# Loading a turn's tile numbers into registers in two halves, in front of their first use

## The chip, the cores and the metric

The kernel runs on one core of a Trainium2 chip. The metric is the device time of the whole program in microseconds (us). Times are medians over runs; a profile is one execution recorded by the hardware profiler. Engines are written as in the profile: PE is TensorE (PEld its weight loads), DVE is VectorE, ACT is ScalarE, POOL is GpSimd, SP is SyncE. A q behind an engine (PEq, PEldq, DVEq, SPq) marks what its sequencer does itself: register work, branches, waits, DMA issues.

## The reference

A graph network of two layers over 6250 nodes with 128 features and 206250 edges. The first layer is a graph attention layer. The second, which the change is about, is this:

```python
msg = jnp.concatenate([x[row], x[col], edge_attr], axis=-1)
h = jax.nn.relu(msg @ W1 + b1)
msg_out = h @ W2 + b2
out = jax.ops.segment_sum(msg_out, row, num_segments=x.shape[0])
```

Here `row` is the source and `col` the target of an edge, and the result is added to x. The kernel splits `msg @ W1` into three parts (source row, target row, edge attributes), and sums the rows after the relu by source node before it multiplies them by W2.

## The kernel before

The program runs in stages. A node stage and an attention stage fill the first 2.2 milliseconds. A target stage then walks the edges in the order of their targets, computes the target and attribute part of each edge's row, and scatters the rows into a table `xr` in DRAM, grouped by the tile of 128 nodes to which the edge's source belongs. Each group is rounded up to 256 rows, so that every block of 256 rows (a pair of 128-row blocks, PR = 2) has sources in a single tile.

The source stage, which the change touches, reads `xr` back in order. There are NPAIR = 856 pairs, eight to a turn (SB = 8), and NTURN = 107 turns. All engines run the same loop over turns, each with its own part, and are tied together by semaphores:

- SP loads two pairs at a time (516 KB) into one of four slots of the buffer `XR` (L423, `load_xr`). The load for a slot waits until ACT has done the relu of the pairs that held it.
- DVE builds the one-hot matrices of a pair (`hotp`, L1342; for the first pair of a slot it also makes the gather's indices, L1333), adds the source part out of PSUM to the pair's rows in XR (`add_r`, L1350), and adds the pair's sums to the running sum of its node tile, `accB[reg]` (`add_up`, L1356).
- PE turns the one-hot matrices (`turnp`, L1679), multiplies them by the node tile's rows `Pt[reg]`, kept as three bf16 parts (`source_rows`, L1688: three matmuls for the second pair of a slot, six for the first), and multiplies the relu's rows by the one-hot matrix to sum them by node (`segment`, L1698: two f32 matmuls, each of which the profile shows as two).
- ACT copies the turned one-hots out of PSUM (L764), widens the other one-hots to f32 (L771) and computes the relu (`relu`, L780).
- POOL adds, for the second block of each second pair, the source part by an indirect DMA from `p_tab` (`source_add`, L556).

PE's loop is staggered: in step m of a turn it runs `turnp(m)`, `source_rows(m-1)`, `segment(m-3)`. DVE's runs `hotp(m+1)`, `add_r(m-2)`, `add_up(m-4)`. ACT's runs the copies of pair m and `relu(m-2)`.

Which node tile a pair belongs to is known only at run time. The numbers stand in one row of on-chip memory, `pbrow`, with four words of zeros ahead of them, so that word p + 4 belongs to pair p. PE and DVE need the number in a register to address `Pt[reg]` and `accB[reg]`. `pair_bins` (its load is L252 in the profile, an instruction TENSOR_LOAD) reads SB + 4 = 12 words at the head of each turn on both engines, the four numbers before the turn and the turn's own eight. PE uses 8 of the 12 (`regs[m + 3]`), DVE the first 8 (`regs[m]`). The loop's own branch and counter are L1712 on PE and L1372 on DVE. A helper of the same kind, `bins` (L246), reads 26 words a batch in the attention stage on PE and DVE; SP reads 7 words at a time at L318.

Of the kernel before, what the change touches and what calls it, by code (L numbers as in the profile page):

```python
# [10 lines left out]
ENG = mybir.EngineType  # L11
# [9 lines left out]
NT = -(-N // P)  # L21
# [23 lines left out]
SB = CP * NS  # L45
NPAIR = -(-((E + NT * (GR - 1)) // GR) // SB) * SB
NTURN = NPAIR // SB
# [18 lines left out]
def gnn(nc, x, src, dst, ea, W, asrc, adst, bias, W1, b1, W2, b2, out):  # L66
# [12 lines left out]
    with ctx:  # L79
# [4 lines left out]
        def sem(name):  # L84
            if name not in sems:
                sems[name] = ctx.enter_context(nc.semaphore(name))
            return sems[name]
# [126 lines left out]
        pbrow = Region(PB0, E1)([NPAIR + 16], I32, 1)  # L214
# [14 lines left out]
        def flat(v):  # L229
            d = dims(len(v.shape) - 1)  # L230
            return v.rearrange(f"p {d} -> p ({d})") if len(v.shape) > 2 else v
# [12 lines left out]
        def bins(engine, b, count):  # L244

            return nc.values_load_multi_w_load_instructions(  # L246
                bin_row[0:1, bass.ds(b * RB, count)], engines=[engine], min_val=0, max_val=NT - 1,
                skip_runtime_bounds_check_because="a node's tile, clamped at 0")[1]

        def pair_bins(engine, i):  # L250

            return nc.values_load_multi_w_load_instructions(  # L252
                pbrow[0:1, bass.ds(i * SB, SB + 4)], engines=[engine], min_val=0, max_val=NT - 1,
                skip_runtime_bounds_check_because="counted over the bins, held under their number")[1]


# [544 lines left out]
        def _(dve):  # L801
# [236 lines left out]
            def add_up(b, t, regs):  # L1038
                dve.wait_ge(sem("agg_ready"), b * BT + t + 1)
                dve.wait_ge(sem("acc_done"), b * (BT + 1) + 2 + t)  # L1040
                a = flat(acc[:, bass.ds(regs[t], 2), :])
                V.tensor_tensor(a, a, PSB[3 + t % 2][:, 0:2 * H * MW], ALU.add).then_inc(sem("acc_done"), 1)  # L1042
# [285 lines left out]
            def hotp(i, m, first):  # L1328
                s, k, g = m // CP, m % CP, SB * i + m
                if k == 0:  # L1330
                    dve.wait_ge(sem(f"xr_in{s}"), 16 * (i + 1))
                    n = len(NADD[s])
                    V.tensor_scalar(sidx[:, s, CP - n:], XR[:, s, CP - n:, RW + HID + 1], 0.0, None, ALU.max).then_inc(sem("idx_ready"), 1)  # L1333
                if not (first and m < 4):
                    dve.wait_ge(sem("pT_ps"), g - 3)
                    dve.wait_ge(sem("ohp_ready"), g - 3)
                if not first:
                    dve.wait_ge(sem("seg_ps"), g - SB + 1)
                for j in range(PR):
                    c, direct = j * RW + HID, j and added(s, k)  # L1340
                    o = OHp[:, m, j, :] if direct else OHq[:, m % 4, j, :]
                    last = V.tensor_scalar(o, iota[:, 0:P] if direct else iotab[:, 0:P], XR[:, s, k, c:c + 1], None, ALU.is_equal)  # L1342
                last.then_inc(sem("ohq_ready"), 1)

            def add_r(g, m, first):
                s, k = m // CP, m % CP
                dve.wait_ge(sem("pp_ps"), g + 1)
                n = PR - added(s, k)
                v = XR[:, s, k, :].rearrange("p (j w) -> p j w", j=PR)[:, 0:n, 0:HID]
                V.tensor_tensor(v, v, PSB[2 + m % 2][:].rearrange("p (j h) -> p j h", j=PR)[:, 0:n, :], ALU.add).then_inc(sem("hp_ready"), 1)  # L1350
# [5 lines left out]
                V.tensor_tensor(a, a, PSB[4 + m % 2][:, 0:XW], ALU.add).then_inc(sem("accB_done"), 1)  # L1356

            def sources(i, first=False, last=False):
                regs = pair_bins(ENG.DVE, i)
                for m in range(SB):  # L1360
                    if m < SB - 1:
                        hotp(i, m + 1, first)
                    else:
                        if not last:
                            hotp(i + 1, 0, False)
                    if not (first and m < 2):
                        add_r(SB * i + m - 2, (m - 2) % SB, first)
                    if not (first and m < 4):
                        add_up(SB * i + m - 4, (m - 4) % SB, regs[m])
            hotp(0, 0, True)  # L1370
            sources(0, True)
            with dve.Fori(1, NTURN - 1) as i:  # L1372
                sources(i)
            sources(NTURN - 1, last=True)
            regs = pair_bins(ENG.DVE, NTURN)
            for m in range(SB - 4, SB):
                if m < SB - 2:
                    add_r(NPAIR - SB + m + 2, m + 2, False)
# [21 lines left out]
        def _(pe):  # L1400
# [92 lines left out]
            regs = bins(ENG.PE, 0, BT)  # L1493
# [10 lines left out]
            regs = bins(ENG.PE, 1, BT)  # L1504
# [171 lines left out]
            def turnp(g, m):  # L1676
                pe.wait_ge(sem("ohq_ready"), g + 1)
                for j in range(PR - added(m // CP, m % CP)):
                    last = pe.transpose(PSB[m % 2][:].bitcast(BF16)[:, j * P:(j + 1) * P], OHq[:, m % 4, j, :], identb)  # L1679
                last.then_inc(sem("pT_ps"), 1)  # L1680

            def source_rows(g, m, reg, first):
                pe.wait_ge(sem("pT_ready"), g + 1)
                if not (first and m < 2):
                    pe.wait_ge(sem("hp_ready"), g - 1)
                for j in range(PR - added(m // CP, m % CP)):
                    for part in range(3):
                        last = pe.matmul(PSB[2 + m % 2][:, j * HID:(j + 1) * HID], ohTp[:, m % 2, j, :],  # L1688
                                         flat(Pt[:, bass.ds(reg, 1), part, :]), start=(part == 0), stop=(part == 2))
                last.then_inc(sem("pp_ps"), 1)  # L1690

            def segment(g, m, first):
                pe.wait_ge(sem("ohp_ready"), g + 1)
                pe.wait_ge(sem("hid_ready"), g + 1)
                if not (first and m < 2):
                    pe.wait_ge(sem("accB_done"), g)
                for j in range(PR):
                    last = pe.matmul(PSB[4 + m % 2][:, 0:XW], OHp[:, m, j, :], hid[:, m % 2, j, :], start=(j == 0), stop=(j == PR - 1))  # L1698
                last.then_inc(sem("seg_ps"), 1)

            def sources(i, first=False):
                regs = pair_bins(ENG.PE, i)
                for m in range(SB):
                    turnp(SB * i + m, m)
                    if not (first and m < 1):
                        source_rows(SB * i + m - 1, (m - 1) % SB, regs[m + 3], first)
                    if not (first and m < 3):
                        segment(SB * i + m - 3, (m - 3) % SB, first)
            pe.wait_ge(sem("pb_in"), 16)
            pe.wait_ge(sem("lo_ready"), NT)  # L1710
            sources(0, True)
            with pe.Fori(1, NTURN) as i:  # L1712
                sources(i)
            regs = pair_bins(ENG.PE, NTURN)
            source_rows(NPAIR - 1, SB - 1, regs[3], False)
            for m in range(SB - 3, SB):
                segment(NPAIR - SB + m, m, False)
            pe.wait_ge(sem("accB_done"), NPAIR + 1)
# [44 lines left out]
```

## Time and profile before

| | |
|---|---|
| median of 3 runs | 5817.26 us (5815.58 to 5819.93) |
| span of the profiled execution, first to last instruction | 5814.8 us |
| source stage, from the first to the last loop branch of PE | 4472.5 to 5770.8 us, 105 turns |
| busy in the span | PE 89%, PEld 70%, DVE 69%, ACT 50%, POOL 68% |
| TensorE's granted clock in the source stage | 1.00 |

The profiler gives no other time for the profiled execution than its span. The span lies inside the runs' times, about 2.5 us under their median. Register, branch, semaphore and DMA-issuing instructions are not counted as busy, so what a sequencer does shows only where a line or an idle gap is looked up.

### The profile page before, as it was taken

To read this page: it belongs to the slowest core of one execution; us is meant where nothing else is said; L and a number is where in the kernel's file an instruction comes from. 1 tells how busy PE (TensorE), PEld (TensorE's weight loads), DVE (VectorE), ACT (ScalarE), POOL (GpSimd) and SP (SyncE) were. 2 spreads that over 40 slices of the span, in tenths; PEclk is the share of its full clock that TensorE was granted. 3 is DMA by queue.
4 is the path that set the end of the run, shared out by engine and by line. 5 is a ranking of instruction groups with operands and counts; after the bars stand their busy time and mean duration, and the time that the engine had idled before them with its cause. 6 is when DMAs were issued, how large, how long until landed. Compare 5 with 4: busy or idle time off the path is not lost.

```text
span 5814.8 us, 160505 instructions
## 1 busy us (share of the span) xinstructions
PE 5152.1 (89%) x34498; PEld 4062.4 (70%) x34499; DVE 3991.1 (69%) x14406; ACT 2887.5 (50%) x8241; POOL 3967.9 (68%) x3713
## 2 busy tenths in 40 slices
PE   4888888888888886999999999999997999999999
PEld 3777777777777764776666666666665777777777
DVE  6788788778778777554455455544545888888887
ACT  3555555555555553333333333332224777777776
POOL 4777777777777774777777777777776555555543
PEclk6888898888888887999999999999998999999999
DMA  4422222222222244998888898888886998999997
GB/s 109 160 53 52 53 52 52 53 52 53 52 53 52 53 118 135 278 264 255 251 253 252 253 256 253 253 259 251 256 252 183 214 213 212 213 214 216 214 210 190
DMA packets 859988, 990.83 MB, mean 170 GB/s; under 512 B 307992, under 2 KB 663224, under 8 KB 859774
## 3 DMA queue, kind: packets, MB, share of 16 engines
q1 hardware_dynamic: 662494, 608.23, 39.9%
q0 software_dynamic: 190592, 378.22, 23.8%
q10 hardware_dynamic: 6816, 3.38, 0.2%
q8 instruction: 37, 0.61, 0.0%
q14 instruction: 49, 0.40, 0.0%
HBM read 726.65 MB, written 262.76 MB: 170 GB/s over the span
## 4 chain that ended last, share of the span: by engine, by line
PE 59%; POOL 11%; issue 11%; DMA 10%; DVE 5%; ACT 2%; DVEq 1%; POOLq 0%; ACTq 0%; SPq 0%
PE bank L1698 13%; PE bank L1530 12%; PE bank L1621 8%; PE bank L1623 7%; PE bank L1688 7%; DMA xr<-arena 7%; POOL arena L494 6%; POOL xr L542 5%; PE bank L1456 2%; DMA arena<-h_tab,arena 2%; PE bank L1679 1%; PE bank L1611 1%; PE bank L1592 1%; PE bank L1466 1%; DVE arena L935 1%
## 5 line engine op out<-in xcount | busy, mean ns | idle before, releaser
L542 POOL DMA_INDIRECT xr<-arena x1612 | 1623.5, 1007 | 511.9 <-issue 383.3
L494 POOL DMA_INDIRECT arena<-h_tab,arena x1612 | 1601.5, 994 | 543.8 <-issue 406.3
L1530 PE MATMUL bank<-arena 128*128 128x136 f32 x6448 | 1321.1, 334 | 76.4 <-DVE arena L1042 9.0
L703 ACT ACTIVATE arena<-bank 128x256 f32<-128x256 f32 x1612 | 594.5, 385 | 1443.1 <-PE bank L1623 986.2
L1621 PE MATMUL bank<-arena 128*128 128x256 f32 x3224 | 1040.1, 405 | 109.8 <-DVE arena L1236 62.0
L556 POOL DMA_INDIRECT arena<-p_tab,arena x428 | 667.8, 1560 | 660.2 <-DMA arena<-p_tab,arena 427.5
L1530 PEld LDWEIGHTS bank<-arena 128*128 128x128 f32 x6448 | 989.2, 216 | 160.5 <-issue 62.1
L621 ACT ACTIVATE arena<-bank 128x256 bf16<-128x256 bf16 x1612 | 618.4, 384 | 922.4 <-PE bank L1456 848.8
L1623 PE MATMUL bank<-arena 128*128 128x256 f32 x3224 | 986.1, 388 | 0.0
L1698 PE MATMUL bank<-arena 128*128 128x257 f32 x3424 | 898.2, 384 | 3.9 <-ACT arena L780 2.7
L1042 DVE TENSOR_TENSOR arena<-arena,bank 128x272 f32 x1612 | 690.7, 428 | 169.5 <-PE bank L1530 156.5
L1236 DVE TENSOR_SCALAR arena<-arena 128x128 f32<-128x128 bf16 x1612 | 464.6, 304 | 448.9 <-PE bank L1623 432.5
L1621 PEld LDWEIGHTS bank<-arena 128*128 128x128 f32 x3224 | 550.4, 203 | 214.5 <-issue 85.9
L1623 PEld LDWEIGHTS bank<-arena 128*128 128x128 f32 x3224 | 631.2, 196 | 91.8
L628 ACT ACTIVATE arena<-arena 128x256 f32<-128x256 bf16 x1612 | 644.9, 408 | 24.9 <-PE bank L1530 21.8
L1698 PEld LDWEIGHTS bank<-arena 128*128 128x128 f32 x3424 | 585.5, 191 | 75.5 <-issue 5.9
L780 ACT ACTIVATE arena<-arena 128x512 f32<-128x512 f32 x856 | 535.5, 626 | 97.1 <-DVE arena L1350 75.0
L1688 PE MATMUL bank<-arena 128*128 x3852 | 567.1, 274 | 2.2 <-DVE arena L1350 1.2
L1456 PE MATMUL bank<-arena 128*128 128x128 bf16 x3224 | 496.9, 241 | 78.9 <-DVE arena L935 72.6
L935 DVE TENSOR_SCALAR arena<-arena 128x256 bf16<-128x256 bf16 x1612 | 466.3, 293 | 143.3 <-issue 136.1
L1350 DVE TENSOR_TENSOR arena<-arena,bank 128x512 f32<-128x512 f32 x856 | 467.1, 546 | 1.7 <-PE bank L1688 1.7
L1342 DVE TENSOR_SCALAR arena<-arena 128x128 bf16<-128x128 bf16 (+1 forms) x1712 | 372.0, 261 | 120.1 <-PE bank L1698 73.3
(253 smaller groups left out, 6450.3 us busy)
## 6 DMA issues: line engine op xcount, KB each, us to landing
arena<-xr SPq DMA_DIRECT2D x428, 516.0 KB, 3.9
arena<-q_tab SPq DMA_DIRECT2D x1612, 128.0 KB
arena<-in_edge_attr SPq DMA_DIRECT2D x61, 832.0 KB
arena<-rel_tab SPq DMA_DIRECT2D x124, 224.0 KB
arena<-h_tab,arena POOLq DMA_INDIRECT x1612
xr<-arena POOLq DMA_INDIRECT x1612
arena<-rel_tab SPq DMA_DIRECT2D x124, 192.0 KB
xr<-arena SPq DMA_DIRECT2D x26, 516.0 KB
```

Source lines behind the costliest of these rows:

```text
L494: pool.indirect_dma_start(G[:, q, t, :], None, h_tab, bass.IndirectOffsetOnAxis(ap=idx[:, q, t:t + 1], axis=0)).then_inc(sem(f"gath{q}"), 16)
L542: pool.indirect_dma_start(xr, bass.IndirectOffsetOnAxis(ap=pos[:, q, t:t + 1], axis=0), Rb[:, t, :], None).then_inc(sem(f"scat{m}"), 16)
L556: pool.indirect_dma_start(XR[:, s, k, RW:RW + HID], None, p_tab, bass.IndirectOffsetOnAxis(ap=sidx[:, s, k:k + 1], axis=0), compute_op=ALU ...
L621: A.activation(ohT[:, (t + 2 * q) % 4, :], PSB[t % 2][:].bitcast(BF16)[:, 0:2 * P], ACT.Copy).then_inc(sem("ohT_ready"), 1)
L628: A.activation(OH[:, (t + 2 * q) % 4, :], OHb[:, q, t, :], ACT.Copy).then_inc(sem("wide_ready"), 1)
L1042: V.tensor_tensor(a, a, PSB[3 + t % 2][:, 0:2 * H * MW], ALU.add).then_inc(sem("acc_done"), 1)
L1456: last = pe.transpose(PSB[t % 2][:].bitcast(BF16)[:, k * P:(k + 1) * P], OHb[:, s, t, k * P:(k + 1) * P], identb)
L1530: last = pe.matmul(PSB[3 + t % 2][:, k * H * MW:(k + 1) * H * MW], OH[:, (t + 2 * q) % 4, k * P:(k + 1) * P], flat(msg[:, t, :, :]), start ...
L1621: pe.matmul(o, OHT[:, (t + 2 * q) % 4, :], Qw[:, t, :], start=True, stop=False)
L1623: pe.matmul(o, EAT[:, (t // 2 + q) % 2, :], w1z[:, t % 2, :], start=False, stop=True).then_inc(sem("main_done"), 1)
L1688: last = pe.matmul(PSB[2 + m % 2][:, j * HID:(j + 1) * HID], ohTp[:, m % 2, j, :], flat(Pt[:, bass.ds(reg, 1), part, :]), start=(part == 0 ...
L1698: last = pe.matmul(PSB[4 + m % 2][:, 0:XW], OHp[:, m, j, :], hid[:, m % 2, j, :], start=(j == 0), stop=(j == PR - 1))
```

## The change

`pair_bins` takes the first pair and a count instead of a turn. PE and DVE no longer load 12 numbers at the head of a turn. Each loads four in step m = 0 and four in step m = 4. On PE the load stands behind `turnp(m)` and in front of `source_rows(m-1)`, and reads the numbers of pairs m-1 to m+2. On DVE it stands behind `add_r(m-2)` and in front of `add_up(m-4)`, and reads those of pairs m-4 to m-1. The loads behind the loop read one word on PE and four on DVE.

```diff
-        def pair_bins(engine, i):
+        def pair_bins(engine, first, count):
...
-                pbrow[0:1, bass.ds(i * SB, SB + 4)], engines=[engine], min_val=0, max_val=NT - 1,
+                pbrow[0:1, bass.ds(first + 4, count)], engines=[engine], min_val=0, max_val=NT - 1,
...
             def sources(i, first=False, last=False):
-                regs = pair_bins(ENG.DVE, i)
                 for m in range(SB):
...
                     if not (first and m < 2):
                         add_r(SB * i + m - 2, (m - 2) % SB, first)
+                    if m % 4 == 0 and not (first and m == 0):
+                        regs = pair_bins(ENG.DVE, SB * i + m - 4, 4)
                     if not (first and m < 4):
-                        add_up(SB * i + m - 4, (m - 4) % SB, regs[m])
+                        add_up(SB * i + m - 4, (m - 4) % SB, regs[m % 4])
...
-            regs = pair_bins(ENG.DVE, NTURN)
+            regs = pair_bins(ENG.DVE, NPAIR - 4, 4)
...
             def sources(i, first=False):
-                regs = pair_bins(ENG.PE, i)
                 for m in range(SB):
                     turnp(SB * i + m, m)
+                    if m % 4 == 0:
+                        regs = pair_bins(ENG.PE, SB * i + m - 1, 4)
                     if not (first and m < 1):
-                        source_rows(SB * i + m - 1, (m - 1) % SB, regs[m + 3], first)
+                        source_rows(SB * i + m - 1, (m - 1) % SB, regs[m % 4], first)
...
-            regs = pair_bins(ENG.PE, NTURN)
-            source_rows(NPAIR - 1, SB - 1, regs[3], False)
+            regs = pair_bins(ENG.PE, NPAIR - 1, 1)
+            source_rows(NPAIR - 1, SB - 1, regs[0], False)
```

## Rows read from the trace of the kernel before

**Rows 1.** Source stage, one window: length, busy by engine, PEclk, DMA share, GB/s

```profile
4472.50:5770.80 1298.30, 1279.31 (x8401) 1009.88 (x8400) 1056.44 (x3778) 959.67 (x2520) 655.07 (x420) 1.00 0.91 214
```

**Rows 2.** The loop branch of PE, line L1712: ns min/median/max, first and last start

```profile
L1712 PEldq COMPARE_BRANCH  x106: 76/208/208, 4472.6 to 5770.8; - x106
```

**Rows 3.** The chain of waits over one turn: start, length, what

```profile
5203.83 0.23 issue
5204.07 0.28 PE bank L1679 x2
...
5204.83 1.07 PE bank L1698 x4
...
5207.48 0.11 PE bank L1679 x2
...
5207.91 0.87 PE bank L1698 x4
5208.79 0.06 PE bank L1679
...
5209.50 0.87 PE bank L1698 x4
...
5216.22 0.28 PE bank L1679 x2
```

**Rows 4.** PE's and DVE's sequencers at that turn's head: L1712, L252, L1677

```profile
L1712 PEldq ALU_OP  x1: 32/32/32, 5202.4 to 5202.4; - x1
L252 PEldq TENSOR_LOAD <-arena x1: 980/980/980, 5202.9 to 5202.9; - x1
L252 DVEq TENSOR_LOAD <-arena x1: 851/851/851, 5203.1 to 5203.1; - x1
L1677 PEldq ALU_OP  x2: 32/34/36, 5204.0 to 5204.8; - x2
```

**Rows 5.** Register loads of 12, 26 and 7 words, over the whole span

```profile
L252 PEldq TENSOR_LOAD <-arena x108: 844/855/1277, 4412.6 to 5771.0; - x108
L246 PEldq TENSOR_LOAD <-arena x62: 2100/2105/4765, 91.2 to 2136.4; - x62
L318 SPq TENSOR_LOAD <-arena x7: 1147/2727/3127, 2139.5 to 2182.2; - x7
```

**Rows 6.** The wait of PE's sequencer ahead of a segment, L1696, in that turn

```profile
L1696 PEldq EVENT_SEMAPHORE  x7: 277/360/445, 5205.7 to 5214.2; - x7
```

**Rows 7.** DVE in order of time around the turn's head

```profile
5204.19 0.45 DVE L1342 TENSOR_SCALAR arena<-arena 128x128 bf16<-128x128 bf16 x2 [0.94 <-PE bank L1698]
5204.55 0.68 DVE L1350 TENSOR_TENSOR arena<-arena,bank 128x512 f32<-128x512 f32 x1
```

**Rows 8.** Two half turns of one buffer's round, in order of time: ACT, SP, DVE

```profile
5203.04 0.63 ACT L780 ACTIVATE arena<-arena 128x512 f32<-128x512 f32 x1 [0.22 <-DVE arena L1350]
...
5203.84 0.37 SPq L423 DMA_DIRECT2D arena<-xr  x1
...
5207.97 0.15 DVE L1333 TENSOR_SCALAR arena<-arena 128x1 int32<-128x1 f32 x1
...
5208.36 0.41 DVE L1350 TENSOR_TENSOR arena<-arena,bank 128x256 f32<-128x256 f32 x1
...
5209.25 0.62 ACT L780 ACTIVATE arena<-arena 128x512 f32<-128x512 f32 x1
...
5214.11 0.15 DVE L1333 TENSOR_SCALAR arena<-arena 128x1 int32<-128x1 f32 x1 [0.27 <-DMA arena<-xr]
...
5215.26 0.63 ACT L780 ACTIVATE arena<-arena 128x512 f32<-128x512 f32 x1
```

**Rows 9.** Landing of the XR loads, and DVE's wait for them, from 4600 us to 5750 us

```profile
DMA to landing us min/median/max: 3.5/3.9/5.9
...
DVE arena L1333 <- DMA arena<-xr: 74.1, 159, 1.6
```

## The prediction

> **What bounds the kernel now.** I read the stretch of the source stage first. From PE's first loop branch to its last it takes 1298 us, with PE busy for 1279, DVE for 1056, the DMA engines at a share of 0.91 and TensorE's clock granted in full (1.00) [rows 1]. The branch starts at 4472.6 us the first time and at 5770.8 the 106th, so a turn of eight pairs takes 1298.2 / 105 = 12.36 us on average [rows 2].
>
> The chain of waits, read next, runs through PE almost without a break. Away from the head, a pair with three source matmuls takes 5208.79 - 5207.48 = 1.31 us and one with six takes 5209.50 + 0.87 - 5208.79 = 1.58 [rows 3]. Four of each make 11.56 us. This turn, from 5204.07 to 5216.22, took 12.15 [rows 3]. So 0.59 us go at the head of an undisturbed turn, and 0.80 on average; 107 turns lose 107 x 0.80 = 85 us. That is all that an edit at the head can win, and the forecast is a share of it.
>
> What happens there is seen at the sequencer. It starts the loop's counter at 5202.4, while PE's array still has work until 5203.83 [rows 3, 4], so it is about 1.4 us ahead. The branch and what goes with it take until 5202.9; then TENSOR_LOAD holds the sequencer for 0.98 us, and `turnp` of the new turn is reached at 5204.0, when the array is already empty [rows 4]. The idle gap of 0.23 us is the smaller part. A sequencer without lead then issues the pair's transposes and three source matmuls in 0.76 us (5204.07 to 5204.83), where an ordinary pair needs 0.43 (5207.48 to 5207.91), and the segment takes 1.07 for 0.87 [rows 3]. DVE loses 0.94 us at the same place, behind its own load of 0.85 [rows 4, 7].
>
> **What the change costs and saves.** *The load itself.* One load of 12 words becomes two of 4. No row shows a load of 4. Twelve words take 0.855 us and 26 take 2.105 on the same engine [rows 5], 0.071 and 0.081 us a word. A price in proportion gives 0.28 to 0.33; the straight line through the two gives 0.855 - 8 x 0.0893 = 0.14, which is the lower bound. Upwards, SP's 7 words took 1.15 at best, on another engine behind its own DMA issues [rows 5], so a fixed part can't be excluded; the upper bound is 0.855, no dearer than 12. I take 0.3, since the two loads on PE leave no room for a fixed part that is large. On PE the block starts three words off a multiple of four, and if that cost a second access it would be about 0.57.
>
> The Trainium skill, page "DMA: Bandwidth & Descriptors", section "Latency and other measured facts", gives a register load a floor of about 600 ns. The 12 and 26 words here fit no such floor with one price a word, since 0.6 us and 0.021 a word would make 26 words 1.15 and not 2.105; by the page a load would be an estimated 0.6 us, the lead at the head would be all but used up, longer loads would stall there, and the sum would be nearer to 12.15 us a turn, 22 us saved.
>
> *PE at the head.* Of the lead of 1.4 us, the branch takes 0.5 as before, which leaves 0.9. Issuing the two transposes takes about 0.2 and gives the array 0.11 of work. A load of 0.3 with an address operation, about 0.1, leaves 0.4. So no gap, and the pair is no longer paced by issue: the whole 0.59 comes back. A load of 0.57 still leaves 0.1. At 0.855 the lead is gone by 0.15, and the pacing (0.33 and 0.20) returns too: then nearly nothing is won at the head.
>
> *PE in the middle (m = 4).* There is no branch there, and the sequencer stands still anyway: ahead of seven of the eight segments it waits 0.28 to 0.45 us for the relu [rows 6]. A load of 0.3 to 0.57 takes the place of this wait. Without that cover it would cost what the head does.
>
> *DVE.* The load leaves the loop head and comes behind `add_r` of a first pair, which runs 0.68 us [rows 7]; 0.3 to 0.6 us of load runs under it. The 0.94 us at the head comes back. Behind the load on DVE's queue stands `add_up`, whose sum is asked for only by a segment one step later. DVE's busy time, 1056 / 105 = 10.06 us a turn [rows 1], is no bound.
>
> *What is late next: the round of the XR buffers.* A load of two pairs waits for a relu, DVE's one-hots wait for its landing, `add_r` follows them in DVE's queue, and the relu behind that lets the load of the slot after next go. Two such half rounds make a turn. In the rows: relu done at 5203.04 + 0.63 = 5203.67, load issued at 5203.84, one-hots begun at 5207.97, relu done at 5209.25 + 0.62 = 5209.87; then one-hots at 5214.11, for which DVE had waited 0.27 on the landing, and relu done at 5215.26 + 0.63 = 5215.89 [rows 8]. The turn's round took 12.22 us, about PE's own 12.15. Little in it is slack. In the first half the relu began 0.48 us after `add_r` ended (5208.36 + 0.41 = 5208.77 to 5209.25) behind ACT's copies for a pair that PE turned late; 0.13 would do, and 0.35 comes back with PE. The first landing may have been up to 0.2 before its use, as the median landing is 3.9 us [rows 9] and the use came 4.13 after the issue. So the round can do 12.22 - 0.35 - 0.2 = 11.67 at a median landing. But landings go from 3.5 to 5.9, and DVE waited for 159 of 372 in this stretch, 74 us in all [rows 9]; lateness in this round adds up, since nothing in it runs ahead. I take 11.85 for it.
>
> *Sum.* PE can do 11.6, the round 11.85. The mean turn now stands 0.21 above its undisturbed one (12.36 to 12.15); I keep 0.2 for that scatter, which makes 12.05. Saved: 12.36 - 12.05 = 0.31 us, in 106 turns 33 us. The stage's first and last turn and the single loads behind the loop change nothing that counts. The profiled span, 5814.8 us, lies 2.5 under the median of the runs, and the difference carries over: 5817.3 - 33 = 5784.
>
> **The rivals.** *The round does not bind.* The landings fall out earlier once the loads are spread evenly, and PE sets the pace alone: 11.56 to 11.7 us a turn, which saves 0.66 to 0.80, 70 to 85 us: 5732 to 5747. For it, PE is busy 1279 of 1298 us; against it, DVE waits for landings already and the DMA share rises from 0.91 to 0.91 x 12.36 / 11.6 = 0.97.
>
> *A load of 4 is as long as one of 12.* Then the change does not do what it is said to: the stall moves behind two transposes and stays. What is won is 0 to 0.1 us a turn: 5806 to 5817. The row of 7 words on SP speaks for it, the two loads on PE against it.
>
> *Slower: the second load is exposed.* If a load holds the sequencer for 0.85 us and the lead at m = 4 is smaller than that, `source_rows(3)` comes late, and the turn pays 0.59 twice: 11.56 + 1.18 + 0.21 = 12.95, 0.59 more than now, 5817 + 63 = 5880. It decides from the point at which a load costs each place more than half of today's loss, 0.4 us. Against it, the waits of [rows 6] stand at just this place.
>
> **How the numbers follow.** The forecast (turn of 11.8 to 12.25 us, 5758 to 5805) gets 0.60, the round not binding, with what lies between, 0.15, the load as long as before 0.17, the exposed second load 0.08. A measurement of this kernel can tell about 0.2%, 12 us, from no change. Faster by more than that: 0.60 + 0.15 = 0.75; within it 0.17; slower 0.08. The likeliest case's own range is 5758 to 5805. To leave out no more than 2 in 10 the range goes from 5752, where most of the second case is left out, to 5815, which takes in most of the third.
>
> **What would show it.** Right: two loads a turn on each of PE and DVE, of about 0.3 us; at the head neither DVE's 0.94 nor PE's issue gap, and the first pair back at 1.31; a mean turn near 12.05, with DVE's wait for the XR landings grown from 74 us. Wrong: loads near 0.85 with the gap behind the transposes; or a turn of 11.6 with no more waiting for landings; or issue gaps ahead of L1688 in the middle of the turn.

## The result and the profile after

The changed kernel takes 5840.57 us (5837.82 to 5851.43, 4 runs) against 5816.42 us of the kernel before on the same chip (4 runs): a ratio of 1.0052 (95% interval 1.004 to 1.0064). It is slower by 24 us, where 33 us less were forecast, and outside the range. One of the ten runs of experiment 8 below had a lower granted clock than all others (0.816 where they had 0.922 or more) and took 5911.42 us; it is left out.

Where the time went is read from the same views as before. First the source stage in one window, then PE's loop branch:

```profile
4468.90:5795.60 1326.70, 1286.93 (x8400) 1026.79 (x8399) 1091.35 (x3781) 935.79 (x2520) 649.86 (x420) 1.00 0.90 209
```

```profile
L1714 PEldq COMPARE_BRANCH  x106: 76/208/208, 4468.9 to 5795.6; - x106
```

A turn now takes (5795.6 - 4468.9) / 105 = 12.635 us, 0.271 more than the 12.364 of [rows 2]; that is 28.5 us over the 105 turns. The stage begins 3.7 us earlier and what follows the loop is 0.3 us shorter, which leaves the 24.5 us by which the span grew, to 5839.3. So all of it is in the turns. The clock is granted in full as before, and the DMA share stands at 0.90 for 0.91 [rows 1].

The register loads, on PE and on DVE:

```profile
L252 PEldq TENSOR_LOAD <-arena x215: 313/1000/1513, 4445.1 to 5795.8; - x108
L252 DVEq TENSOR_LOAD <-arena x214: 340/345/448, 4450.3 to 5795.7; - x107
```

Here the forecast breaks. Four words take 0.345 us on DVE and 1.000 us on PE, where twelve took 0.855 [rows 5]. The shortest on PE, 0.313 us, is the single word behind the loop.

PE in order of time over one turn's head and middle (start, length, in brackets the idle time before):

```profile
5203.34 0.27 PE L1680 MATMUL bank<-arena 128*128 128x128 bf16 x2
5203.94 0.53 PE L1689 MATMUL bank<-arena 128*128 x3 [0.33 <-DVE arena L1350]
5204.44 1.13 PE L1699 MATMUL bank<-arena 128*128 128x257 f32 x4
5205.41 0.22 PE L1680 MATMUL bank<-arena 128*128 128x128 bf16 x1
...
5206.99 0.27 PE L1680 MATMUL bank<-arena 128*128 128x128 bf16 x2
...
5208.30 0.22 PE L1680 MATMUL bank<-arena 128*128 128x128 bf16 x1
...
5209.88 0.27 PE L1680 MATMUL bank<-arena 128*128 128x128 bf16 x2
5210.12 0.53 PE L1689 MATMUL bank<-arena 128*128 x3
5210.50 1.11 PE L1699 MATMUL bank<-arena 128*128 128x257 f32 x4
5211.44 0.22 PE L1680 MATMUL bank<-arena 128*128 128x128 bf16 x1
```

The pair at the head takes 5205.41 - 5203.34 = 2.07 us and the pair at m = 4 takes 5211.44 - 5209.88 = 1.56, where an ordinary one takes 5208.30 - 5206.99 = 1.31. That is 0.76 + 0.25 = 1.01 us a turn, against the 0.59 of the turn of [rows 3] and the 0.80 of the mean one. It is a typical turn: counted in this way over 103 turns of the trace, from the third to the 105th, the two pairs take 2.09 and 1.59 us in the mean, and all others their 1.31 and 1.58. PE's sequencer at the same two places:

```profile
L1714 PEldq ALU_OP  x1: 32/32/32, 5202.1 to 5202.1; - x1
L252 PEldq TENSOR_LOAD <-arena x1: 999/999/999, 5202.7 to 5202.7; - x1
L1686 PEldq ALU_OP  x1: 36/36/36, 5203.7 to 5203.7; - x1
...
L1678 PEldq ALU_OP  x1: 32/32/32, 5208.6 to 5208.6; - x1
L252 PEldq TENSOR_LOAD <-arena x1: 1002/1002/1002, 5208.8 to 5208.8; - x1
L1686 PEldq EVENT_SEMAPHORE  x1: 51/51/51, 5209.9 to 5209.9; - x1
```

The load starts at 5202.7 and the sequencer comes to `source_rows` (L1686) at 5203.7, behind it. The transposes in front of the load went through without a gap, as the change wants it; the source matmuls have to wait. The view puts the 0.33 us down to DVE's L1350, which ended shortly before. But from the end of the load to the first source matmul it is 0.27 us in nearly every turn of the trace, here from 5203.67 to 5203.94, and 0.28 at m = 4, where the view shows no wait for DVE. So the load sets the time, and experiments 1 and 2 test it.

### The profile page after: what moved, and what is told of

Its sections match the earlier page's. It is cut to its first block, busy times and chain, and to the rows that moved or that the text cites. A ratio compares the mean times of both kernels' runs of the same rounds, so it can differ in the third digit from the quotient of the medians.

```text
span 5839.3 us, 160929 instructions
## 1 busy us (share of the span) xinstructions
PE 5147.5 (88%) x34498; PEld 4071.0 (70%) x34499; DVE 4021.6 (69%) x14406; ACT 2859.9 (49%) x8241; POOL 3956.6 (68%) x3713
## 4 chain that ended last, share of the span: by engine, by line
PE 53%; DMA 12%; issue 12%; POOL 11%; DVE 8%; DVEq 2%; ACT 2%; POOLq 0%; ACTq 0%; SPq 0%
PE bank L1531 11%; PE bank L1699 9%; PE bank L1622 8%; PE bank L1624 7%; DMA xr<-arena 7%; POOL arena L494 5%; PE bank L1689 5%; POOL xr L542 5%; DMA arena<-xr 3%; PE bank L1457 2%; DMA arena<-h_tab,arena 2%; PE bank L1612 1%; DVE arena L935 1%; DVE arena L1042 1%; PE bank L1593 1%
## 5 line engine op out<-in xcount | busy, mean ns | idle before, releaser
L621 ACT ACTIVATE arena<-bank 128x256 bf16<-128x256 bf16 x1612 | 616.9, 383 | 920.0 <-PE bank L1457 839.9
L764 ACT ACTIVATE arena<-bank 128x256 bf16<-128x256 bf16 x856 | 282.4, 330 | 406.3 <-PE bank L1680 395.8
L1350 DVE TENSOR_TENSOR arena<-arena,bank 128x512 f32<-128x512 f32 x856 | 468.6, 547 | 1.9 <-PE bank L1689 1.9
```

What stands on the lines that cost most here:

```text
L621: A.activation(ohT[:, (t + 2 * q) % 4, :], PSB[t % 2][:].bitcast(BF16)[:, 0:2 * P], ACT.Copy).then_inc(sem("ohT_ready"), 1)
```

## The experiments

The experiments ran on two other chips, on which the kernel before had a median of 5810.33 us (beside experiments 1 to 4) and 5809.33 (beside 5 to 8), 13 runs each. That is 6 to 7 us less than on the chip of the result, so savings are compared here and not bare times. A turn is worked out as above, from PE's loop branch. A load is called in line where its first word is a multiple of four of its row, and out of line elsewhere; the kernel starts each row at a multiple of eight words of its on-chip buffer.

**1. The row stored one word further on.** PE's loads begin at word 8i + 3 or 8i + 7 of the row, DVE's at 8i or 8i + 4. Theory A: the first word's place sets the price. Theory B: the place in PE's queue does.

```diff
-                pbrow[0:1, bass.ds(first + 4, count)], engines=[engine], min_val=0, max_val=NT - 1,
+                pbrow[0:1, bass.ds(first + 5, count)], engines=[engine], min_val=0, max_val=NT - 1,
...
-            sp.dma_start(pbrow[:, 4:4 + NPAIR], pb_tab[0:NPAIR].rearrange("(a n) -> a n", a=1)).then_inc(sem("pb_in"), 16)
+            sp.dma_start(pbrow[:, 5:5 + NPAIR], pb_tab[0:NPAIR].rearrange("(a n) -> a n", a=1)).then_inc(sem("pb_in"), 16)
```

> The row of tile numbers is stored one word further on, and both engines read it one word further on; all else is as in the changed kernel. In the changed kernel PE's loads of four words begin at words 3 and 7 of a turn and took 1.0 us, DVE's begin at words 0 and 4 and took 0.34. Theory A, the address: a load is dear when its first word is not a multiple of four. Then the two swap, PE's loads near 0.34 us and DVE's near 1.0. PE's gaps at m = 0 and m = 4 go, DVE's load sticks out 0.3 us behind add_r twice a turn: a turn near 12.1 to 12.3, 5790 to 5815 us. Theory B, the place: PE's load is long because it stands behind transposes in PE's queue. Then PE's stays at 1.0 and DVE's at 0.34, 5840 us.

The loads, then the wait of DVE's `add_up` behind its load from 4600 to 5650 us (us in total, times, longest):

```profile
L252 PEldq TENSOR_LOAD <-arena x215: 312/350/942, 4436.4 to 5726.3; - x108
L252 DVEq TENSOR_LOAD <-arena x214: 959/966/1364, 4441.3 to 5726.3; - x107
...
DVE arena L1356 <- issue: 49.6, 115, 0.7
```

The two prices swapped: 0.350 us on PE and 0.966 on DVE. Theory B falls. The time is 5775.68 us, a ratio of 0.9944 (0.9926 to 0.9963). That saves 35 us, where 27 (5790 for 5817) were expected at best, and the turn is (5726.2 - 4460.1) / 105 = 12.06 us. So one word's shift turns a loss of 0.5% into a gain of 0.6%, and DVE bears a load of nearly 1 us twice a turn almost without harm to the turn, though it waits behind it.

**2. Both aligned**, that is, in line. PE gets a copy of the row of its own, one word further on, in words that the target stage no longer needs.

```diff
+        pbrow2 = Region(WORDS - NB * RB)([NPAIR + 16], I32, 1)
...
-                pbrow[0:1, bass.ds(first + 4, count)], engines=[engine], min_val=0, max_val=NT - 1,
+                (pbrow2 if engine == ENG.PE else pbrow)[0:1, bass.ds(first + (5 if engine == ENG.PE else 4), count)], engines=[engine], min_val=0, max_val=NT - 1,
...
             load_windows(NB - 1, 1, part=NT - 1)
+            sp.dma_start(pbrow2[:, 5:5 + NPAIR], pb_tab[0:NPAIR].rearrange("(a n) -> a n", a=1)).then_inc(sem("pb_in"), 16)
...
-            dve.wait_ge(sem("pb_in"), 16)
+            dve.wait_ge(sem("pb_in"), 32)
...
-            pe.wait_ge(sem("pb_in"), 16)
+            pe.wait_ge(sem("pb_in"), 32)
```

> PE reads its own copy of the row, stored one word further on, so that its loads begin at a multiple of four words; DVE keeps its row. Theory A: both loads near 0.34 us, no gap at the head or in the middle of the turn. If the round of the XR buffers then binds, as the prediction had it, a turn of 12.05 us and 5784 us, with DVE waiting more for landings; if PE sets the pace alone, 11.6 to 11.7 and 5735 to 5750. Theory B: PE's load stays at 1.0, 5840 us.

The loads, the branch, DVE's waits from 4600 to 5650 us (us in total, times, longest) and the landings of the XR loads in that stretch:

```profile
L253 PEldq TENSOR_LOAD <-arena x215: 313/337/767, 4448.8 to 5732.6; - x108
L253 DVEq TENSOR_LOAD <-arena x214: 339/344/657, 4453.6 to 5732.5; - x107
...
L1716 PEldq COMPARE_BRANCH  x106: 76/208/208, 4471.0 to 5732.5; - x106
...
DVE arena L1335 <- DMA arena<-xr: 134.3, 269, 1.9
...
DMA to landing us min/median/max: 3.6/4.0/5.1
```

The time is 5772.53 us, a ratio of 0.9933 (0.9914 to 0.9952): ahead of both kernels, and the lowest median of the versions that compute the whole result, though experiments 1 and 6 lie within its interval. The turn is (5732.5 - 4471.0) / 105 = 12.01 us, and the forecast for a load of 0.3 us had been 12.05. DVE waits twice as long for landings as in the kernel before, whose row for the same stretch is:

```profile
DVE arena L1333 <- DMA arena<-xr: 67.5, 147, 1.6
```

**3. A list of prices, first try.** Twenty loads of 1 to 16 words ahead of the source stage on PE, each on a line like this one:

```diff
             pe.wait_ge(sem("lo_ready"), NT)
+            nc.values_load_multi_w_load_instructions(pbrow[0:1, 17:21], engines=[ENG.PE], min_val=0, max_val=NT - 1, skip_runtime_bounds_check_because='a price')
```

> The kernel before, with twenty register loads of 1 to 16 words from different first words run once on PE, ahead of the source stage, each on a line of its own. Theory A: four words cost 0.34 us from words 0 and 4 and about 1.0 from words 1, 2 and 3; 12 words cost 0.85 from word 0 and more from word 3. Theory B: the first word makes no difference; four words cost 0.34 from anywhere. The loads add some 10 to 15 us to the time, which says nothing else.

It measured nothing: the trace holds no load from those lines. Nothing used the registers, which is the likely reason, but that was not followed up. 5815.48 us, one run. Experiment 7 is the second try.

**4. DVE's part alone.** PE loads twelve words at the head, as before. `four` is the `pair_bins` of the changed kernel under another name; the load behind the loop changes in the same way and is not shown.

```diff
             def sources(i, first=False, last=False):
-                regs = pair_bins(ENG.DVE, i)
...
+                    if m % 4 == 0 and not (first and m == 0):
+                        regs = four(ENG.DVE, SB * i + m - 4, 4)
                     if not (first and m < 4):
-                        add_up(SB * i + m - 4, (m - 4) % SB, regs[m])
+                        add_up(SB * i + m - 4, (m - 4) % SB, regs[m % 4])
```

> DVE's part of the change alone: PE still loads twelve words at the head. DVE's gap of 0.94 us at the head goes. Theory: the head's loss on the path is PE's, so a turn loses only the lateness that DVE's gap causes later in it, 0.05 to 0.15 us of the 0.80: 5800 to 5812 us. Rival: DVE's gap is part of what empties PE at the head: 5770 to 5800.

5800.26 us, a ratio of 0.9985 (0.9975 to 0.9996), and a turn of (5754.4 - 4468.3) / 105 = 12.25 us, 0.11 less. The bare time lies on the border that the expectation drew between theory and rival. It drew that border for the 5817 us of the other chip, though; the saving of 10 us lies within the theory's 5 to 17 and short of the rival. PE's first pair of a turn takes 1.69 us in the mean, counted as above, just as in the kernel before. So DVE's part alone leaves the loss at PE's head where it was.

**5. The gathers left out.** POOL's gathers of the source stage and the relu's wait for them are taken out of experiment 2.

```diff
-            pool.wait_ge(sem("p_out"), 16 * NT)
-            for s in range(NS):
-                source_add(0, s)
-            with pool.Fori(1, NTURN) as i:
-                for s in range(NS):
-                    source_add(i, s)
...
-                if added(s, k):
-                    act.wait_ge(sem(f"gath{s % 2}"), GSUM + 16 * len(NADD[s]) * (c + 1))
```

> The kernel with both loads aligned (turn 12.00 us), and POOL's gathers in the source stage left out with the relu's wait for them, so the second block of every second pair lacks its source part. This takes 27% of the source stage's DMA time away and nothing from PE, DVE or ACT. Theory: the round of the XR buffers sets the turn, so with the landings down from about 4.1 to about 3.5 us the turn falls until PE binds, 11.6 to 11.75 us. Rival: PE's head sets the turn (its pair 0 takes 1.57 for 1.31); then it stays at 11.9 to 12.0.

The branch, then DVE's waits and the landings from 4600 to 5650 us:

```profile
L1707 PEldq COMPARE_BRANCH  x106: 76/208/211, 4441.1 to 5665.1; - x106
...
DVE arena L1326 <- DMA arena<-xr: 0.6, 3, 0.2
...
DMA to landing us min/median/max: 3.2/3.6/4.0
```

The median landing falls from 4.0 to 3.6 us, DVE's wait for it from 134 to 0.6 us, and the turn to (5665.1 - 4441.1) / 105 = 11.66 us; 5706.63 us in all, a ratio of 0.9823 (0.9807 to 0.9839). PE, DVE and ACT have the work of experiment 2, and PE and DVE its loads. What is left at PE's head costs about 0.1 us over the 11.56 that the pairs need: the first pair takes 1.40 us in the mean, where it took 1.57 in experiment 2. So half of what comes back, 0.17 us, shows at the head, though PE's instructions there are the same.

The edit takes away more than late landings: POOL's work goes too, and so does a lengthening of some of PE's loads (last section). The trace of experiment 2 tells these apart as far as it can. The 71 of its 103 turns in which PE's load at the head took under 0.36 us still take 11.94 in the mean. DVE's `add_r` has the same lengths in both runs, 0.41 and 0.68 us. The quarter of the turns in which DVE waited least for landings takes 11.75 us, and the quarter in which it waited most 12.23. So most of what stands between 12.01 and 11.66 goes with the landings; it was not tested with POOL's work left in place.

**6. Two turns an iteration on PE.**

```diff
-            with pe.Fori(1, NTURN) as i:
-                sources(i)
+            with pe.Fori(0, NTURN // 2) as i:
+                sources(2 * i + 1)
+                sources(2 * i + 2)
```

> The kernel with both loads aligned, PE's loop running two turns an iteration, so that every second turn has no branch (0.5 us of the sequencer's time). Theory (the round binds): the turn stays at 11.95 to 12.05, and what the head no longer loses turns up as waits elsewhere. Rival (PE's head binds): half of the 0.26 us lost at the head comes back, 11.87 us, some 14 us faster than with one turn an iteration.

5775.94 us, a ratio of 0.9938 (0.9921 to 0.9954), which is experiment 2's within the intervals. The branch comes 53 times, from 4474.9 to 5732.2 us, so a turn is 1257.3 / 104 = 12.09 us. Half of the branches are worth nothing, as the theory of the round of the buffers has it.

**7. A list of prices, second try.** One load a pair on each engine in place of those at the heads, two of them shown here and the others as listed below:

```diff
+                    if m == 0:
+                        reg = nc.values_load_multi_w_load_instructions(pbrow[0:1, bass.ds(SB * i + 0, 16)], engines=[ENG.DVE], min_val=0, max_val=NT - 1, skip_runtime_bounds_check_because='a price')[1][0]
+                    if m == 1:
+                        reg = nc.values_load_multi_w_load_instructions(pbrow[0:1, bass.ds(SB * i + 1, 8)], engines=[ENG.DVE], min_val=0, max_val=NT - 1, skip_runtime_bounds_check_because='a price')[1][0]
...
-                        add_up(SB * i + m - 4, (m - 4) % SB, regs[m])
+                        add_up(SB * i + m - 4, (m - 4) % SB, reg)
```

> The kernel before with the loads at the heads replaced by one load a pair on each engine, of many lengths and first words, each on a line of its own; the registers used hold the right numbers. Theory (a load is split into accesses of four words where it starts at a multiple of four, and into single words where it doesn't): 0.31 for 1 word anywhere, about 0.34 for 2 to 4 aligned words, 0.57 for 8, 0.85 for 12, 1.1 for 16; out of line about 0.24 a word: 2 words 0.5, 3 words 0.75, 4 words 1.0, 8 words 2.0, 12 words 2.9. Rival (only one access more for crossing a boundary of four words): out of line 0.3 more than aligned, 8 words 0.85, 12 words 1.1; but then 4 words would be 0.6 and not 1.0. The time of the whole only shows that loads stall.

The loads, DVE's first (L1368 to L1382), then PE's (L1720 to L1734), ns min/median/max:

```profile
L1368 DVEq TENSOR_LOAD <-arena x106: 1102/1108/1116, 4462.3 to 6280.3; - x106
L1370 DVEq TENSOR_LOAD <-arena x106: 1854/1857/2241, 4464.3 to 6282.0; - x106
L1372 DVEq TENSOR_LOAD <-arena x106: 536/957/1004, 4466.9 to 6284.7; - x106
L1374 DVEq TENSOR_LOAD <-arena x106: 2719/2724/3109, 4468.4 to 6286.0; - x106
L1376 DVEq TENSOR_LOAD <-arena x107: 850/853/1319, 4454.1 to 6289.2; - x107
L1378 DVEq TENSOR_LOAD <-arena x107: 737/740/756, 4455.8 to 6290.6; - x107
L1380 DVEq TENSOR_LOAD <-arena x107: 1843/2208/2280, 4458.1 to 6292.0; - x107
L1382 DVEq TENSOR_LOAD <-arena x107: 598/602/641, 4460.8 to 6294.5; - x107
...
L1720 PEldq TENSOR_LOAD <-arena x106: 307/311/327, 4461.5 to 6279.7; - x106
L1722 PEldq TENSOR_LOAD <-arena x107: 298/304/312, 4449.5 to 6281.1; - x107
L1724 PEldq TENSOR_LOAD <-arena x107: 539/543/685, 4450.6 to 6282.5; - x107
L1726 PEldq TENSOR_LOAD <-arena x107: 537/733/857, 4451.6 to 6285.4; - x107
L1728 PEldq TENSOR_LOAD <-arena x107: 1002/1007/1338, 4453.3 to 6287.0; - x107
L1730 PEldq TENSOR_LOAD <-arena x107: 997/1000/1266, 4455.8 to 6289.8; - x107
L1732 PEldq TENSOR_LOAD <-arena x107: 598/600/951, 4457.6 to 6291.7; - x107
L1734 PEldq TENSOR_LOAD <-arena x107: 780/819/1259, 4459.2 to 6293.1; - x107
```

| words | in line, median us | out of line, median us (words past a multiple of four) |
|---|---|---|
| 1 | 0.304 (L1722) | 0.311 (L1720, three) |
| 2 | 0.543 (L1724) | 0.733 (L1726, one), 0.957 (L1372, two) |
| 3 | 0.819 (L1734) | 0.740 (L1378, one) |
| 4 | 0.344 (DVE, experiment 2) | 1.000 (L1730, one), 1.007 (L1728, two) |
| 8 | 0.600 (L1732), 0.602 (L1382) | 1.857 (L1370, one), 2.208 (L1380, two) |
| 12 | 0.853 (L1376) | 2.724 (L1374, three) |
| 16 | 1.108 (L1368) | |

In line, each whole group of four words costs 0.25 us on top of 0.09. All other words cost some 0.21 to 0.24 each, on top of the same 0.09; the two and three words of a short load in line too, for which the expectation had 0.34. Three loads out of line were dearer than this in most turns, both of two words and the one of eight that starts two past (2.208, where 0.09 + 8 x 0.23 gives 1.93), for a reason that no run looks into. The rival, one access more for a crossing, gave 0.85 for 8 words out of line and 1.1 for 12: they took at least 1.86 and 2.72. The price of 26 words in [rows 5] fits too, six groups and two words: 0.09 + 6 x 0.25 + 2 x 0.23 = 2.05, for 2.105 measured. The kernel as a whole took 6337.99 us (one run), which says no more than that loads stall.

**8. PE's part alone, aligned.** PE as in experiment 2, here with `four` reading PE's own copy of the row; DVE loads twelve words at the head.

```diff
             def sources(i, first=False):
-                regs = pair_bins(ENG.PE, i)
                 for m in range(SB):
                     turnp(SB * i + m, m)
+                    if m % 4 == 0:
+                        regs = four(ENG.PE, SB * i + m - 1, 4)
```

> PE's part of the change alone, with aligned loads from its own copy of the row; DVE loads twelve words at the head as before. DVE's part alone gave a turn of 12.23 for 12.36 us, both gave 12.00. Theory: PE's head loss goes, but DVE's gap of 0.94 us at the head now delays the round of the XR buffers: 12.1 to 12.2 us, 5785 to 5797. Rival: DVE's part is worth nothing beside PE's: 12.0 us, 5772.

The nine runs have a median of 5800.81 us (5795.72 to 5811.26), and the ratio is 0.9992 (0.9982 to 1.0002): not clear of no difference, and less of a gain than even the theory expected. The turn is (5748.9 - 4458.6) / 105 = 12.29 us. The chain of waits over one turn's head says why (start, length, what):

```profile
5203.25 4.45 DMA arena<-xr
...
5208.43 0.03 issue
5208.46 0.06 DVEq L1380
5208.52 0.14 issue
5208.65 0.18 DVE arena L1364
5208.84 0.04 issue
5208.88 0.85 DVEq L259
```

With PE's stall gone, the chain runs over a landing of the XR load to DVE, and 0.85 us of DVE's own twelve-word load (L259) stand on it. PE meets that in the pair behind the first, which takes 2.00 us in the mean, counted as above, for 1.58. By the ratios, DVE alone saves 2 to 15 us, PE alone up to 10 and perhaps nothing, both 28 to 50: each part hides some of what the other would gain.

## Why the prediction was wrong

**The step that failed is the price of the load.** "I take 0.3, since the two loads on PE leave no room for a fixed part that is large", with an upper bound of 0.855, "no dearer than 12". On DVE four words took 0.345 us; on PE 1.000, above the bound. The two rows that it rested on, 12 and 26 words, both begin at a multiple of four, and so could not show what a load out of line costs. The next sentence even saw the block's start "three words off a multiple of four" and priced it as one access more, 0.57. Experiments 1 and 7 show a price of about 0.23 us for each of the words instead, (1.000 - 0.09) / 4. That twelve is an upper bound for four was an assumption and not a reading. The sum that the forecast gave by the Trainium skill (page "DMA: Bandwidth & Descriptors", section "Latency and other measured facts"), whose floor for a `tensor_load` is about 600 ns, starts from a price that these loads don't have either: one word took 0.304 us and four in line 0.344.

**The head.** The lead at the branch and what the branch takes came out as forecast: the counter starts at 5202.1, the load 0.6 us later, and the transposes run without a gap. At a load of 1.0 us the lead is gone by the prediction's own count (0.9 - 0.2 + 0.11 - 1.1, 0.3 short), and the idle gap of 0.33 us and the pacing of three matmuls and a segment are what the profile shows.

**The middle of the turn.** The cover was right for a load of 0.3 us and too small for one of 1.0. The load does take the place of one of the waits of [rows 6], that ahead of the segment of the same step. Here is that wait in the kernel before and in the changed one, in the turns shown above:

```profile
L1696 PEldq EVENT_SEMAPHORE  x1: 336/336/336, 5209.6 to 5209.6; - x1
...
L1697 PEldq EVENT_SEMAPHORE  x1: 51/51/51, 5210.4 to 5210.4; - x1
```

That gives back 0.29 us of the 1.0. But `source_rows(3)` stands between the load and this wait, and for it the only cover is the lead of the queue, from 5208.6 to the transposes at 5209.88. A load of 1.0 us uses all of it, and 0.25 us is lost; with one of 0.34 the pair is back at 1.31 in the mean (experiment 5). So the last of the rivals, an exposed second load, is what happened, at 0.25 us where it was priced at 0.59.

**DVE.** Right as far as it went: behind the load of 0.345 us `add_up` shows no such wait as in experiment 1, neither in the changed kernel nor in experiment 2, and even at 0.966 the turn is only 0.05 us longer than in experiment 2. That DVE's gap has to go together with PE's was not in the forecast (experiments 4 and 8).

**The round of the XR buffers.** Late landings are what is left, as forecast, though the changed kernel can't show it. With the load at the price that the forecast assumed, the turn is 12.01 us for a forecast 12.05, DVE's wait for landings doubles, and experiment 5 takes that wait away and gives 11.66. Experiment 6 finds nothing to win at the branch. The rival without the round (11.56 to 11.7) falls for the kernel with its gathers.

That 12.01 came so near to 12.05 is in part luck. The forecast added 11.85 for a steady round and 0.2 for scatter, and the runs don't show these two terms. In experiment 2, 32 of the 103 turns take 11.64 to 11.67 us, which is the time of a turn with the gathers left out, and late turns make the mean. The 0.2 was the distance of the mean from a turn of 12.15; that is the shortest that the kernel before shows, and its median turn takes 12.23.

## What to carry to other kernels

Before a register load is split or moved, look at the remainder of its first word by four: four words in line cost 0.34 us and out of line 1.0, more than twelve in line (0.85). Where a load lies in front of an engine's work, compare its length with the time from the sequencer's last step to the work still queued, at that place, after the waits that stand ahead of it. And bound an unseen operation by rows that differ from it in every respect that the change alters, its address too, not only in its length.

## What the runs showed of the hardware

A register load on PE or DVE whose first word is a multiple of four costs 0.09 us and 0.25 for each whole group of four words; every other word costs some 0.21 to 0.24 by itself, and in three of the loads out of line more (experiment 7). Below four words there is no group: one word costs 0.304, two in line 0.543 and three 0.819, so four (0.344) are cheaper than two. PE's aligned loads are also lengthened in some turns: up to 0.767 us in experiment 2, yet never over 0.345 with the gathers left out, where the row is

```profile
L253 PEldq TENSOR_LOAD <-arena x215: 315/333/345, 4418.2 to 5665.2; - x108
```

That the gathers lengthen them is what this suggests; no run here takes it further.
